# Two convolution layers with group normalisation: the sums between the passes computed another way

## What is computed

```python
def _gn(v, G=4, eps=1e-5):
    B_, C_, H_, W_ = v.shape
    g = v.reshape(B_, G, C_ // G, H_, W_)
    m = jnp.mean(g, axis=(2, 3, 4), keepdims=True)
    s = jnp.var(g, axis=(2, 3, 4), keepdims=True)
    return ((g - m) / jnp.sqrt(s + eps)).reshape(v.shape)

x = x + _L0_conv_ref(_gn(x), L0_conv_weight, L0_conv_bias)
x = x + _L1_conv_ref(_gn(x), L1_conv_weight, L1_conv_bias)
```

## Time and profile before

| | us |
|---|---|
| median of three runs | 3963.27 |
| the profiled execution, its own time | 3966.73 |
| its span, first to last instruction | 3965.1 |
| busy: TensorE matmul / VectorE / ScalarE / GpSimd | 3489.6 / 1430.5 / 1710.2 / 590.8 |
| DMA, mean over the span | 339 GB/s (1344.32 MB) |
| granted TensorE clock, mean | 0.964 |

### The profile page before, as it was taken

One profiled execution on the slowest core, in us unless ns is written; L12 is line 12 of the kernel. 1 busy time (PEld: TensorE's weight loads), 2 busy tenths in 40 slices (PEclk: granted clock), 3 DMA queues, 4 the chain that ended last, 5 costly groups with the idle time before them and its releaser, 6 DMA issues. The chain is left out here.

```text
span 3965.1 us, 217004 instructions
## 1 busy us (share of the span) xinstructions
PE 3489.6 (88%) x99136; PEld 1836.0 (46%) x99136; DVE 1430.5 (36%) x2460; ACT 1710.2 (43%) x1553; POOL 590.8 (15%) x1061
## 2 busy tenths in 40 slices
PE   0797999979899798997989989898898979999898
PEld 0353554435454354544544445443454435555454
DVE  6555114541245411553125531255313552223300
ACT  0343544434444344443444435454344434544344
POOL 0111111111111111111111111111111111111111
PEclk9998999989999899998999989999999999999999
DMA  9797999979989798998989989899898998989798
GB/s 344 251 387 283 394 375 337 370 290 387 351 338 371 293 389 305 385 370 303 387 298 390 353 309 390 299 389 355 318 387 300 383 337 331 390 281 312 250 310 270
DMA packets 334124, 1344.32 MB, mean 339 GB/s; under 512 B 38800, under 2 KB 38928, under 8 KB 301200
## 3 DMA queue, kind: packets, MB, share of 16 engines
q10 hardware_dynamic: 149648, 537.60, 39.3%
q0 software_dynamic: 147456, 536.94, 34.5%
q1 hardware_dynamic: 36864, 268.45, 18.8%
HBM read 805.45 MB, written 536.87 MB: 339 GB/s over the span
## 5 line engine op out<-in xcount | busy, mean ns | idle before, releaser
L390 PE MATMUL conv<-x_tile,wts 32*32 32x512 f32 x49152 | 3398.7, 603 | 173.0 <-DMA x_tile<-x_dram 67.9
L395 PE MATMUL conv<-x_tile,wts 32*32 32x512 f32 x49152 | 3421.9, 606 | 2.5 <-issue 2.5
L390 PEld LDWEIGHTS conv<-x_tile,wts 32*32 32x32 f32 x49152 | 1597.1, 103 | 1734.2 <-issue 1424.6
L329 ACT ACTIVATE out_tile<-conv,bias 128x1024 f32<-128x1024 f32 x512 | 570.2, 1114 | 2016.4 <-PE conv L395 1947.6
L454 DVE BATCH_NORM_STATS2 bn_mid<-out_tile 128x6 f32<-128x512 f32 x1024 | 658.0, 685 | 989.8 <-ACT out_tile L329 738.9
L395 PEld LDWEIGHTS conv<-x_tile,wts 32*32 32x32 f32 x49152 | 956.8, 103 | 79.3 <-issue 4.6
L446 DVE BATCH_NORM_STATS2 bn_x<-stat_tile 128x6 f32<-128x512 f32 x896 | 550.6, 680 | 1047.6 <-DMA stat_tile<-x_dram 1047.6
L333 ACT ACTIVATE out_tile<-conv,bias 64x1024 f32<-64x1024 f32 x512 | 568.5, 1110 | 12.9
L331 ACT ACTIVATE out_tile<-conv,bias 64x1024 f32<-64x1024 f32 x512 | 567.0, 1107 | 13.0
L231 POOL DMA_DIRECT2D mid_dram<-out_tile x512 | 273.0, 533 | 1619.5 <-ACT out_tile L329 1129.0
L231 POOL DMA_DIRECT2D out_dram<-out_tile x512 | 268.2, 524 | 1534.9 <-ACT out_tile L329 1063.9
(11 more groups left out here) (45 smaller groups left out, 117.2 us busy)
## 6 DMA issues: line engine op xcount, KB each, us to landing
stat_tile<-x_dram SPq DMA_DIRECT2D x256, 1024.0 KB, 9.9
mid_dram<-out_tile POOLq DMA_DIRECT2D x512, 512.0 KB, 10.4
out_dram<-out_tile POOLq DMA_DIRECT2D x512, 512.0 KB, 9.1
x_tile<-x_dram ACTq DMA_DIRECT2D x504, 512.0 KB, 13.2
x_tile<-mid_dram ACTq DMA_DIRECT2D x504, 512.0 KB, 9.3
x_tile<-x_dram ACTq DMA_DIRECT2D x8, 480.0 KB, 9.7
x_tile<-mid_dram ACTq DMA_DIRECT2D x8, 480.0 KB, 6.2
x_tile<-pad_row ACTq DMA_DIRECT2D x16, 32.0 KB
```

Source lines behind the costliest of these rows:

```text
L329: act.activation(out_tile[:, slot, 0], conv[:, parity, 0], ACT.Identity, bias=bias[:, 0:1]).then_inc(evicted, 1)
L390: nc.tensor.matmul(columns_of(parity, i, q, c), wts[part, MAIN, kw], rows_of(TILE * q, TILE, slot, c, kw), start=first, stop=end)
L395: last = nc.tensor.matmul(columns_of(parity, i, q, 1 - c), wts[part, ABOVE, kw], rows_of(TILE * above, TILE, slot if q else (slot - 1) % S ...
```

## The change

- Late statistics: for the last two units of layer 0 (`LATE`), `take_mid_late` reads the accumulators themselves, second block first, while ScalarE evicts the first; ScalarE waits for `second_taken` before its second instruction. The accumulators lack the bias, so it is added to the mean of that part.
- Aggregation in two parts: the first 30 units' (or tiles') worth (120 of 128 entries of bn_stats) ahead, the last 8 entries in the gap. For x both parts are done right after the last tile. `mv` holds mean and variance of both parts, and a matmul for each part (`sum_parts`, the group matrix times the part's share) adds them into one column: every partition gets its own group's value at once, and the four columns and the choice among them are gone.
- For that, a tile of the statistics of x now holds 16 pairs of rows of all 8 channels (`x_by_pair`: a partition's two rows are 8 KB in one piece, neighbouring partitions lie 4 MB apart in DRAM), instead of 256 rows of one channel.
- The bias: the taps are summed once at the start (`taps_in`, `tap_sum`, `sum_taps`; 32 small copies on GpSimd), and one matmul with mean times scale (`taken`) replaces the 24 with `plain`. `wts` is made in one instruction.
- The pads' side columns and first row go from VectorE to ScalarE (`begin`), on either side of the root.
- GpSimd waits for `wts_ready` instead of `mean_known` before it fills `pad_row`.
- In the first image the larger part is aggregated between tiles 29 and 30, and the loop over tiles ends four tiles earlier, with the tap sums behind it.

```diff
+STAT_PAIRS = STAT_ROWS // CH // 2
+PARTS = UNITS * 2 * HALVES
+LATE = 2
+LATE_PARTS = LATE * 2 * HALVES
+SPLIT_AT = (0, PARTS - LATE_PARTS, PARTS)
+SHARES = (1 - LATE / UNITS, LATE / UNITS)
...
-    x_rows = x.rearrange("n c h w -> (n c h) w")
+    x_by_pair = x.rearrange("n c (h a) w -> h n c (a w)", a=2)
...
                 sp.dma_start(stat_tile[:, s],
-                             x_rows[bass.ds((n * STATS + i) * STAT_ROWS, STAT_ROWS), :]
-                             .rearrange("(p a) w -> p (a w)", p=P)).then_inc(stat_loaded[s], 16)
+                             x_by_pair[STAT_PAIRS * i:STAT_PAIRS * (i + 1), bass.ds(n, 1)]
+                             .rearrange("h n c w -> h (n c) w")).then_inc(stat_loaded[s], 16)
...
-            alone(pool.tensor_scalar(own_group[:, :], same_group[:, 0:CH:GROUP_CH],
-                                     float(ROWS * GROUP_CH), 0.0, ALU.mult, ALU.add))
-            alone(pool.tensor_scalar(mid_group[:, :], same_group[:, 0:CH:GROUP_CH],
-                                     float(ROWS * GROUP_CH * GROUPS), 0.0, ALU.mult, ALU.add))
+            for late in range(2):
+                alone(pool.tensor_scalar(sum_parts[:, late], same_group[:, :], SHARES[late], 0.0,
+                                         ALU.mult, ALU.add))
+            pool.wait_ge(tap_sums, 2)
+            for layer in range(2):
+                part = slice(TILE * layer, TILE * layer + CH)
+                for r in range(ROWS):
+                    alone(pool.tensor_scalar(sum_taps[part, CH * r:CH * (r + 1)], tap_sum[part, :],
+                                             -1.0, 0.0, ALU.mult, ALU.add))
...
-                        pool.wait_ge(mean_known, 2 * n + (g // UNITS + 1))
+                        pool.wait_ge(wts_ready, 2 * n + (g // UNITS + 1))
                         pool.sem_inc(results_seen)
                         pool.tensor_scalar(pad_row[0:CH, :], zeros[0:CH, :], own_mean[0:CH, 0:1],
                                            None, ALU.add).then_inc(pad_row_filled, 1)
...
+            for layer in range(2):
+                act.dma_start(taps_in[TILE * layer:TILE * layer + CH, :],
+                              taps[layer].rearrange("c k t -> c (k t)")).then_inc(setup_loaded, 16)
...
                 act.activation(out_tile[:, slot, 0], conv[:, parity, 0], ACT.Identity,
                                bias=bias[:, 0:1]).then_inc(evicted, 1)
+                if layer == 0 and u >= UNITS - LATE:
+                    act.wait_ge(second_taken, LATE * n + (u - (UNITS - LATE) + 1))
                 act.activation(out_tile[HALF:P, slot, 1], conv[0:HALF, parity, 1], ACT.Identity,
                                bias=bias[0:HALF, 0:1]).then_inc(evicted, 1)
...
+            def begin(n, layer):
+                p = 2 * n + layer
+                act.wait_ge(mean_known, p + 1)
+                act.activation(x_tile[:, :, 0:SIDE + 2:SIDE + 1], ones[:, :, :], ACT.Identity,
+                               scale=own_mean[:, 0:1])
+                act.wait_ge(var_read, p + 1)
+                act.activation(root[:, :], var[:, :], ACT.Sqrt).then_inc(root_done, 1)
+                part = slice(P - TILE, P)
+                act.wait_ge(above_known, p + 1)
+                act.sem_inc(rows_asked)
+                act.wait_ge(head_loaded, 16 * (p + 1))
+                act.activation(x_tile[part, LAST_SLOT, 1:SIDE + 1], head[part, :], ACT.Identity,
+                               bias=above[part, 0:1], scale=is_first[part, 0:1]) \
+                   .then_inc(pads_written, 1)
+                act.wait_ge(wts_ready, p + 1)
...
-                nc.tensor.matmul(conv[:, 0, 0, 0:GROUPS], average[:, :], share[:, :], start=True,
-                                 stop=True).then_inc(mean_summed, 1)
+                for late in range(2):
+                    last = nc.tensor.matmul(conv[:, 0, 0, 0:1], sum_parts[:, late], mv[:, late, 0:1],
+                                            start=(late == 0), stop=(late == 1))
+                last.then_inc(mean_summed, 1)
                 pe.wait_ge(var_share, p + 1)
                 pe.sem_inc(unit_begun)
...
+                for late in range(2):
+                    last = nc.tensor.matmul(conv[:, 0, 0, 0:1], sum_parts[:, late],
+                                            share[:, late:late + 1], start=(late == 0),
+                                            stop=(late == 1))
+                last.then_inc(var_summed, 1)
                 pe.wait_ge(taken_known, p + 1)
                 pe.sem_inc(unit_begun)
...
-                last.then_inc(bias_summed, 1)
+                nc.tensor.matmul(conv[:, 0, 0, 1:2], sum_taps[:, :], taken[:, :], start=True,
+                                 stop=True).then_inc(bias_summed, 1)
...
+            def take_mid_late(n, u):
+                dve.wait_ge(conv_done, units_through(n, u))
+                for i in (1, 0):
+                    if i == 0:
+                        last.then_inc(second_taken, 1)
+                        dve.wait_ge(evicted, evicts_through(n, u, 1))
+                    for h in range(HALVES):
+                        last = dve.bn_stats(bn_mid[:, (2 * u + i) * HALVES + h, :],
+                                            conv[:, u % 2, i, h * BANK:(h + 1) * BANK])
+                last.then_inc(mid_taken, 1)
+            def aggregate(bn, late):
+                return dve.bn_aggr(mv[:, late, :], bn[:, SPLIT_AT[late]:SPLIT_AT[late + 1], :]
+                                   .rearrange("p a b -> p (a b)"))
+            def sums_of(n, layer):
+                p = 2 * n + layer
                 dve.wait_ge(mean_summed, p + 1)
-                after_all(dve.tensor_copy(mean[:, :], conv[:, 0, 0, 0:GROUPS]))
+                after_all(dve.tensor_copy(own_mean[:, :], conv[:, 0, 0, 0:1]))
                 wait_for_all()
...
+                dve.sem_inc(mean_known)
+                after_all(dve.tensor_scalar(shift[:, :], mv[:, :, 0], own_mean[:, 0:1], None,
+                                            ALU.subtract))
                 wait_for_all()
                 after_all(dve.tensor_tensor(shift[:, :], shift[:, :], shift[:, :], ALU.mult))
                 wait_for_all()
...
+                dve.tensor_tensor(share[:, :], shift[:, :], mv[:, :, 1], ALU.add) \
+                   .then_inc(var_share, 1)
+                dve.tensor_tensor(above[:, :], own_mean[:, :], is_above[:, :], ALU.mult) \
+                   .then_inc(above_known, 1)
                 dve.wait_ge(var_summed, p + 1)
-                dve.tensor_scalar(var[:, :], conv[:, 0, 0, 0:GROUPS], EPS, None, ALU.add) \
+                dve.tensor_scalar(var[:, :], conv[:, 0, 0, 0:1], EPS, None, ALU.add) \
                    .then_inc(var_read, 1)
                 dve.wait_ge(root_done, p + 1)
                 after_all(dve.reciprocal(rstd[:, :], root[:, :]))
                 wait_for_all()
...
+                after_all(dve.scalar_tensor_tensor(newton[:, :], rstd[:, :], var[:, 0:1], rstd[:, :],
+                                                   ALU.mult, ALU.mult))
                 wait_for_all()
...
                 after_all(dve.tensor_scalar(newton[:, :], newton[:, :], -0.5, 1.5, ALU.mult, ALU.add))
                 wait_for_all()
+                after_all(dve.tensor_tensor(own_rstd[:, :], rstd[:, :], newton[:, :], ALU.mult))
                 wait_for_all()
...
+                dve.scalar_tensor_tensor(taken[:, :], own_mean[:, :], own_rstd[:, 0:1],
+                                         of_layer[:, layer:layer + 1], ALU.mult, ALU.mult) \
+                   .then_inc(taken_known, 1)
+                dve.scalar_tensor_tensor(wts[:, :, :, :], band[:, layer], own_rstd[:, 0:1],
+                                         ident[:, :, :, :], ALU.mult, ALU.add)
                 dve.wait_ge(bias_summed, p + 1)
+                dve.tensor_scalar(bias[:, :], conv[:, 0, 0, 1:2], bias_col[:, layer:layer + 1], None,
+                                  ALU.add).then_inc(wts_ready, 1)
...
             def image(n, last_image):
                 begun[0] = FOR_IMAGE * n + AT_START
                 steps[0] = 0
-                dve.wait_ge(stat_used, STATS * n + STATS)
-                dve.sem_inc(sums_begun)
                 sums_of(n, 0)
                 for g in range(2 * UNITS):
-                    if g == UNITS:
+                    if g < UNITS - LATE:
+                        take_mid(n, g)
+                    elif g < UNITS:
+                        if g == UNITS - LATE:
+                            dve.wait_ge(mid_taken, UNITS * n + (UNITS - LATE))
+                            dve.sem_inc(sums_begun)
+                            aggregate(bn_mid, 0)
+                        take_mid_late(n, g)
+                    if g == UNITS - 1:
                         dve.wait_ge(mid_taken, UNITS * n + UNITS)
                         dve.sem_inc(sums_begun)
+                        after_all(aggregate(bn_mid, 1))
+                        wait_for_all()
```

(31 more changed lines are left out.)

130 lines of the change are left out of this document (28 added, 102 removed).

## The result

The changed kernel took 4173.57 us (median of 4, 4171.81 to 4184.58), the kernel before 3962.01 (median of 4); ratio 1.054, interval 1.0515 to 1.0559. The profiled execution spans 4170.2 us against 3965.1: 205.1 more, where the forecast had some 65 fewer.

A forecast was written before the change was run, and what follows sets the result against it. TensorE, busy 88%, was taken to bound the kernel, with convolution setting layer 1 passes and loads layer 0's. 3966.7 - 64 - 19 - 2 + 20 = 3902, stated as 3898 because the profiled execution is 3.5 above the median; range 3874 to 3925.

The forecast's parts named there:

- Start of layer 1: Gap before layer 1's first convolution, 8 times: 9.6 us instead of 17.6, 64 us less in all.
- Start of layer 0: Gap from root to convolution at 7 later starts: 2.9 us less at five, 2.1 at two, 19 in all.
- The added wait: ScalarE waiting for `second_taken` at units 30 and 31: covered, price 0; uncovered, at most 2 us at each of 8 places.
- First pass: Before the first convolution, where VectorE sets the end: start at 123.1 us instead of 125.5, 2 us less.
- The statistics' loads: Tiles of x at 4 MB pitch: 18 us over 7 layer 0 passes, about 2 around the first start, together 20.
- the 11%: Extra packet time of row loads of x (0.218 us) over `mid` loads (0.197); half of it was charged to the tiles.
- hidden: Dearer statistics' loads in layer 1 passes cost nothing, since loads reach 419 GB/s and need 376.
- Rival 1: Layer 0 loses what the gaps give: passes go from 224 to 238 us, total 3986, slower than before; 14%.
- Rivals 3 and 4: Layer starts gain only 5 and 1 us, 3934, 17%; layer 0 passes give back their 19 us, 3917, 8%.
- Rival 2: Tiles cost double through lock-stepped reads at one pitch: 48 us more per layer 0 pass, total 4385; 3%.

The follow-up runs named there:

- e1: The changed kernel with the statistics' tiles of x loaded in one piece again (layer 0's groups wrong): 3884.16 us, 0.978 of the kernel before.
- e9: The changed kernel with tiles read as 128 pieces of 8 KB at one even 256 KB step (groups wrong): 3888.84 us, 0.980 of the kernel before.
- e11: e9 with a group matrix for each layer, so the full result is right: 3883.04 us, 0.980 of the kernel before.
- e13: e11 with layer 0's row loads reading 128 pieces that follow each other (wrong rows): 3768.52 us, 0.950 of the kernel before.
- e3: The changed kernel with the tiles' channel pieces 4 MB less 8 KB apart instead of 4 MB: 4176.29 us, 1.052 of the kernel before.
- e7: The changed kernel with each tile one contiguous megabyte, but dealt out as 16 x 8 pieces (groups wrong): 4175.06 us, 1.052 of the kernel before.
- e12: The changed kernel with each tile in eight loads, one per channel, into every eighth partition: 4144.8 us (one run), 1.045 of the kernel before.
- e10: The changed kernel with each tile in eight loads, each into 16 neighbouring partitions (groups wrong): 4871.17 us (one run), 1.23 of the kernel before.
- e4: e1 with layer 0's four columns of sums and two copies of TensorE's loop body, full result: 3977.37 us, 1.003 of the kernel before.
- e8: e4 with TensorE's program as one loop body making both kinds of sums: 3893.82 us, 0.982 of the kernel before.
- e14: e11 with GpSimd filling the pad row at `mean_known` again, as before the change: 3894.92 us, 0.982 of the kernel before.

## Why the prediction was wrong

- Start of layer 1, -64: measured -63.4. Start of layer 0, -19: -19.0. Both hold, and the running sum through the first was never off by more than 0.4 us. The closeness of the totals is in part luck: with the same edits the kernels of the experiments have -63 to -69 and -16 to -22. L509, called a one-column step in the forecast, has four columns.
- The added wait, priced 0: e1's layer 0 passes take 224 to 225 us in the loop, as before. Holds.
- First pass, -2: with fast loads e9, e1 and e11 start 2.5, 3.2 and 4.2 us earlier than before (e11 at 121.28 against 125.48). A little more than was said.
- **"The statistics' loads", +20, is the step that failed: about 290.** The forecast made a tile 5.5% dearer; with the queue full an 8 KB piece took 0.61 us against 0.32, 90% more. It was "This is the part that can turn the sign", and the price was wrong in three ways. First, the 11% came from 4 KB packets "Where nothing else presses", between two kinds of load that also differ in source and in what runs beside them. e13 against e11 changes only the view of the rows, 0.222 against 0.176: 26%. Second, the engines of that stretch were not free: over the 190 us of the earlier trace rows their share over all queues is 0.98 at only 311 GB/s, and in e13 it is 0.82 at 299 (windows below). A packet's time there says little of the rate under pressure, 217 GB/s against 416. Third, "The pieces are twice as long, so I take the half": nothing in the trace said so.

```profile
3520.00:3710.00 190.00, 185.66 (x5411) 101.37 (x5409) 72.41 (x113) 93.99 (x85) 29.77 (x56) 1.00 0.98 311
3320.00:3510.00 190.00, 185.71 (x5388) 101.26 (x5376) 69.86 (x109) 91.52 (x83) 32.11 (x56) 0.99 0.82 299
```

- "hidden" in layer 1 was the second error of the same term: the loads needed 376 GB/s and could do 419. That leaves 209 x (1 - 376/419) = 21 us of room in a pass; 15 tiles that each take 2.4 us longer (4.9 against 1.05 MB at 416 GB/s) are 36, so 15 should show, and 17.2 did.
- Rival 1 priced a layer 0 pass at 238, and 237 to 242 came, but it had the first start at 134 (measured 184) and left layer 1 free. Rivals 3 and 4 fall: the changes of pass gave what was forecast, and e1's layer 0 passes gave nothing back.
- Rival 2 had tiles at double cost and 3%. Its price of a tile was near: 55 forecast ahead of the first pass, 62 measured (after against e1); 16 a pass in layer 1, 17.2 measured. That was luck, since its cause fell with e3 and e7, and its 48 us to a layer 0 pass were 15. Why the two slow kinds of load cost less together than their sum is open; no run was made for it.
- Of the three conditions named for being wrong, layer 0 passes over 232 us and tiles over 3.2 us apart are met; a start of layer 1 over 12 us isn't. The Trainium skill's rule (DMA: Bandwidth & Descriptors, Latency and other measured facts) of the 4 MiB pitch warned of the right place, but its cause is not the one here. By that rule the full rate comes back once the pitch is padded by 4 KiB; here e3 at 4 MB less 8 KB had 218 GB/s and e7 with no pitch at all 219.

## What to carry to other kernels

A load's price must be read where its queue is full, from the same form of load: GB/s at DMA share 1, not packets' time in a stretch where the convolution sets the pace. When a tile's view changes, keep one outer step over the 128 partitions if the data allow it; at 8 KB and at 256 KB distance that alone decided here between 5% slower and 2% faster. Where one term can turn the sign, its upper bound belongs in the range until a row of the same kind rules it out.

## What the runs showed of the hardware

- The DMA share doesn't tell a slow load from a fast one: 1.02 at 217 and at 419 GB/s.
- 8 loads of 128 KB for one of 1 MB, into the same partitions, left the DMA engines idle 37% of the time (e12, 187 to 191 GB/s); into 16 partitions side by side the engines were busy and moved 124 to 131 GB/s (e10).
- Two copies of TensorE's loop body cost some 84 us in all (e4 against e8), at the units just after each switch, where 6 or 8 packets of the instruction queue come each time.
- One step of VectorE (128 x 2) that begins 0.2 us after GpSimd starts on 8 x 1024 numbers takes 0.90 us instead of 0.16; the next ones beside the same 2.84 us of GpSimd do not (e14).
